# The stage before and in a selective scan: the convolution moved ahead of a norm, identity products in waits, and the scan taken quarter by quarter

## The chip, the cores and the metric

One core of a Trainium2 chip runs the whole kernel. The metric is the device time of one execution in microseconds (us), the median of three runs. TensorE multiplies matrices into PSUM, VectorE (DVE) and ScalarE (ACT) work elementwise, GpSimd (POOL) works elementwise in SBUF, and SyncE (SP) issues the DMAs.

## The reference, cut to what matters

Six blocks with a layer norm after each; only the first, a Mamba-like block over x of shape 2 x 256 x 128, is touched:

```python
xn = _ln(x, ln1_g, ln1_b);  xm = _ln(xn, ln_g, ln_b)
x1 = xm @ w1_w + w1_b
xc = silu(depthwise_conv3(x1))                 # over time, per channel
delta = softplus(xc @ dt_w + dt_b)             # [B, T, 128]
Bt, Ct = xc @ Bp_w + Bp_b, xc @ Cp_w + Cp_b    # [B, T, 16]
A = -exp(A_log)                                # [128, 16]
h = exp(delta * A) * h + delta * Bt * xc       # scan over T, 128 x 16 states
y = sum_n h * Ct + D_p * xc
mo = (y * silu(xm @ v1_w + v1_b)) @ w2_w + w2_b
```

The second block attends from x to a context of 2 x 512 x 128, which is normed on its own (`cx`, the norm `ctx`), transposed to `cxnT` and projected to keys and values.

## The kernel before, in words

There are 512 columns (2 batches by 256 steps) and 2048 states, taken as 16 groups (`NG`) of 128 rows. Group (q, i) holds 8 of the 128 channels with 16 states each: channels 32q + 8i to 32q + 8i + 7. The list `ORDER` gives the group of each scan step s.

**Ahead of the scan.** VectorE norms x twice (L773, L776, L783), GpSimd computing each norm's rstd with a power (L488, L490). VectorE then norms the context's eight tiles (`layernorm("ctx", ...)`), and after that computes the convolution in three instructions (L825, L826, L828). TensorE transposes x, multiplies by w1 and v1, transposes the context, and multiplies xc by dt, B and C. ScalarE evacuates (L584, L592), takes the two Silus (L595, L598), the Exp of A_log into `nA` (L599), and the softplus parts Abs, Exp, Ln (L604 to L606). VectorE forms delta (L835) and delta times x (L850), and splits each into three bfloat16 parts (L792 to L801). A quarter q of the channels is then stacked as 96 rows, a part under another (`quads`): quarters 0 and 1 by copies on VectorE (`quad`, L843, three copies for each of delta and dx), quarters 2 and 3 by 12 DMAs (L416), for which step 4 waits.

**A scan step s.** TensorE spreads delta and dx of the group from `quads` over 128 rows (`mm` with `sel_g`, L1190) into banks s % 2 and 2 + s % 2. ScalarE makes dA by Exp (L639). VectorE multiplies the spread dx by B in place (L861) and scans (L866). GpSimd multiplies by C (L509) into one of eight buffers of `hC`. The spread of delta waits for dA of step s - 2, that of dx for the scan of step s - 2. Behind the two spreads TensorE's queue holds, from step 2 on, one `values0`, four 128-column products of the next block, evacuated by ScalarE (L630).

**The sum over states.** `y_of(k)` multiplies four groups' hC by `sel_y` (128 rows to 32 columns of weights) into rows 32q to 32q + 31 of bank 4. The groups are those of `SUMMED[k]`. It stands in TensorE's queue behind the spreads of steps 8, 10 and 14, and the last one behind step 15. Then follow D_p (L870), the gate (L873), w2, the residual and the next norm.

Every float32 matmul shows as two records in the trace.

Of the kernel before, what the change touches and what calls it, by code (L numbers as in the profile page):

```python
# [23 lines left out]
P = 128  # L24
# [5 lines left out]
NC_TILES = B * CS // P  # L30
STATE = 16
GD = P // STATE
NG = D // GD
# [11 lines left out]
PARTS = 3  # L45
# [8 lines left out]
VEC = {}  # L54
# [16 lines left out]
def program(nc, a, out):  # L71
# [3 lines left out]
    with ctx:  # L75
        def sb(name, shape, dt=f32):
            return ctx.enter_context(nc.sbuf_tensor(name, shape, dt))
# [65 lines left out]
        def v(name, i=0, rows=P):  # L143
            at = VEC[name][0] + i
            return vec[0:rows, at:at + 1]

        def rv4(name):
# [95 lines left out]
        t1 = sb("t1", [P, 4, NJ, 8])  # L243
        pr1 = sb("pr1", [P, 2, NJ, 8])
        cmb = sb("cmb", [P, NJ, E1])
        hh = big2(0, [P, C1, N])
        hsh = big1(0, [P, SH, N])

# [22 lines left out]
        S = {k: sem(k) for k in (  # L271
            "w1_ps", "v1_ps", "x1p_done", "conv_done", "xc_done", "gate_done",
            "dt_ps", "z_done", "BC_ps", "BC_done", "negA", "lg_done", "delta_parts", "dx_parts",
            "delta_quads", "dx_quads", "late_quads",
            "spread_d", "spread_x", "dA_done", "dBx_done", "scan_done", "hC_done", "y_ps",
            "yv_done", "mo_ps", "res_ready", "x2_done", "ff_ps", "ff_act", "ff2_ps",
            "cxnT_ps", "cxnT_done",
# [22 lines left out]
        def own(eng, chain):  # L300
# [3 lines left out]
            def link(ins):  # L304
# [4 lines left out]

        ORDER = ([(q, i) for two in ((0, 1), (2, 3)) for i in range(2) for q in two]
                 + [(q, i) for i in (2, 3) for q in range(4)])

        SUMMED = ((0, 1, 4, 5), (2, 3, 6, 7), (8, 9, 10, 11), (12, 13, 14, 15))
        KEYS = {"a": T, "x": CS}

        AHEAD = {"a": 24, "x": 29}
# [70 lines left out]
        def _(sp):  # L389
# [19 lines left out]
            sp.dma_start(eb[:], a["eb"].partition_broadcast(P)).then_inc(ld["e1"], 16)  # L409


            for kind, parts in enumerate(("delta_parts", "dx_parts")):
                for q in (2, 3):
                    for i in range(PARTS):
                        sp.wait_ge(S[parts], i + 1)
                        sp.dma_start(quads[32 * i:32 * i + 32, kind, q, :],  # L416
                                     dparts[32 * q:32 * q + 32, kind, i, :]
                                     ).then_inc(S["late_quads"], 16)

            def spread_max(L):  # L420

# [47 lines left out]
        def _(pool):  # L469
# [32 lines left out]
            for s in range(NG):  # L502
                pool.wait_ge(S["scan_done"], s + 1)
                if s == 0:
                    pool.wait_ge(S["BC_done"], 2)
                if s >= 8:

                    pool.wait_ge(S["y_ps"], 1 if s < 10 else 2)
                nc.gpsimd.tensor_tensor(hC[:, s % 8, :], hs[:, s % 4, :], Cn[:],  # L509
                                        ALU.mult).then_inc(S["hC_done"], 1)  # L510
            root("ln2")
# [63 lines left out]
        def _(act):  # L575
            link = own(act, act_own)

            def to_cols(dst, bank, ready, done, scale=None, bias=None, n=1):

                act.wait_ge(S[ready], n)  # L580
                if scale is None:
                    nc.scalar.activation(dst, ps[:, bank, :], ACT.Copy).then_inc(S[done], 1)
                else:
                    nc.scalar.activation(dst, ps[:, bank, :], ACT.Identity, scale=scale,  # L584
                                         bias=bias).then_inc(S[done], 1)


            act.wait_ge(ld["vec"], 16)
            to_cols(xT[:], 0, "xT_ps", "xT_done", v("ln_g"), v("ln_b"), 1)
            act.wait_ge(S["w1_ps"], 1)  # L590
            act.wait_ge(consts, 9)
# [4 lines left out]
                                 ).then_inc(S["gate_done"], 1)  # L596
            act.wait_ge(S["conv_done"], 1)
            nc.scalar.activation(xc[:], cv[:, 0, :], ACT.Silu).then_inc(S["xc_done"], 1)  # L598
            link(nc.scalar.activation(nA[:, 0, :], vec[:, VEC["A_log"][0]:VEC["A_log"][0] + NG],  # L599
                                      ACT.Exp))  # L600
            nc.scalar.mul(nA[:, 1, :], nA[:, 0, :], -1.0).then_inc(S["negA"], 1)

            act.wait_ge(S["z_done"], 1)
            link(nc.scalar.activation(dtmp[:, 0, :], cv[:, 1, :], ACT.Abs))  # L604
            link(nc.scalar.activation(dtmp[:, 1, :], dtmp[:, 0, :], ACT.Exp, scale=-1.0))
            nc.scalar.activation(dtmp[:, 2, :], dtmp[:, 1, :], ACT.Ln, bias=1.0  # L606
                                 ).then_inc(S["lg_done"], 1)
# [6 lines left out]
            for i in range(2):  # L614
                to_cols(cxnT[:, i * 512:(i + 1) * 512], 6 + i, "cxnT_ps", "cxnT_done",
                        v("ctx_g"), v("ctx_b"), i + 1)
            act.wait_ge(S["negA"], 1)

            def evac0(c, kind):
# [145 lines left out]
        def _(dve):  # L765
            link = own(dve, dve_own)

            def layernorm(name, src, dst, meanwhile=None):

                k = NORMS.index(name)  # L770
                nt = src.shape[1]
                for j in range(nt):
                    ins = nc.vector.bn_stats(stats[:, j, :], src[:, j, :])  # L773
                link(ins)
                for j in range(nt):
                    ins = nc.vector.bn_aggr(meanvar[:, k, j, :], stats[:, j, :])  # L776
                ins.then_inc(norm_var, 1)
                dve.wait_ge(norm_var, k + 1)
                if meanwhile:
                    meanwhile()  # L780
                dve.wait_ge(norm_rstd, k + 1)
                for j in range(nt):
                    nc.vector.tensor_scalar(dst[:, j, :], src[:, j, :], meanvar[:, k, j, 0:1],  # L783
                                            rstd[:, k, j:j + 1], ALU.subtract, ALU.mult
                                            ).then_inc(norm_out, 1)
                dve.wait_ge(norm_out, normed_tiles(name))
# [16 lines left out]
            def gather_fours(L, fs=range(H // 4)):  # L803

                for f in fs:
                    for i in range(PARTS):
# [10 lines left out]
            layernorm("ln", summed[:], normed)  # L817

            dve.wait_ge(ld["cx"], 16)
            layernorm("ctx", cx, cx)  # L820

            dve.wait_ge(ld["vec"], 16)
            dve.wait_ge(S["x1p_done"], 1)
# [3 lines left out]
                                                cv3[:, 0], ALU.mult, ALU.add))  # L827
            nc.vector.scalar_tensor_tensor(cv3[:, 0], x1p[:, :, 2:T + 2], v("conv", 2), cv3[:, 1],  # L828
                                           ALU.mult, ALU.add).then_inc(S["conv_done"], 1)
            dve.wait_ge(S["dt_ps"], 1)  # L830
            nc.vector.tensor_scalar(cv[:, 1, :], ps[:, 3, :], v("dt_b"), None, ALU.add
                                    ).then_inc(S["z_done"], 1)
            dve.wait_ge(S["z_done"], 1)
            dve.wait_ge(S["lg_done"], 1)
            link(nc.vector.scalar_tensor_tensor(dl[:, 0, :], cv[:, 1, :], 0.0, dtmp[:, 2, :],  # L835
                                                ALU.max, ALU.add))
            split(dl[:, 0, :], [dparts[:, 0, i, :] for i in range(3)], dtmp[:, 0, :],
                  S["delta_parts"])

            def quad(kind, q, done):  # L840

                for i in range(PARTS):
                    ins = nc.vector.tensor_copy(quads[32 * i:32 * i + 32, kind, q, :],  # L843
                                                dparts[32 * q:32 * q + 32, kind, i, :])
                ins.then_inc(S[done], 1)

            dve.wait_ge(S["delta_parts"], PARTS)
            quad(0, 0, "delta_quads")
            dve.wait_ge(S["xc_done"], 1)
            link(nc.vector.tensor_tensor(dl[:, 1, :], dl[:, 0, :], xc[:], ALU.mult))  # L850
            split(dl[:, 1, :], [dparts[:, 1, i, :] for i in range(3)], dtmp[:, 1, :], S["dx_parts"])
            dve.wait_ge(S["dx_parts"], PARTS)
            quad(1, 0, "dx_quads")
            quad(0, 1, "delta_quads")
            quad(1, 1, "dx_quads")

            dve.wait_ge(S["BC_done"], 1)
            for s in range(NG):
# [329 lines left out]
        def _(pe):  # L1188
# [8 lines left out]
            def to_cols(bank, src, done, norm=None):  # L1197

                for j in range(NJ):
                    if norm:  # L1200
                        pe.wait_ge(norm_out, normed_tiles(norm, j))
                    ins = nc.tensor.transpose(ps[:, bank, j * P:(j + 1) * P], src[:, j, :], ident[:])  # L1202
                ins.then_inc(S[done], 1)
# [8 lines left out]


            pe.wait_ge(ld["ident"], 16)
            to_cols(0, normed, "xT_ps", "ln")
            pe.wait_ge(ld["mix"], 16)
            pe.wait_ge(S["xT_done"], 1)
            mm(ps[:, 1, :], w_mix[:, 0, :], xT[:]).then_inc(S["w1_ps"], 1)
            mm(ps[:, 2, :], w_mix[:, 1, :], xT[:]).then_inc(S["v1_ps"], 1)
            pe.wait_ge(norm_out, normed_tiles("ctx"))  # L1220
            for i in range(2):
                to_cols(6 + i, cx[:, 4 * i:4 * i + 4, :], "cxnT_ps")
            pe.wait_ge(S["xc_done"], 1)
            mm(ps[:, 3, :], w_mix[:, 2, :], xc[:]).then_inc(S["dt_ps"], 1)
            mm(ps[:, 4, :], w_mix[:, 3, :], xc[:])
            mm(ps[:, 5, :], w_mix[:, 4, :], xc[:]).then_inc(S["BC_ps"], 1)

            pe.wait_ge(ld["sel"], 32)
            pe.wait_ge(S["delta_parts"], PARTS)
# [46 lines left out]

            for s, (q, i) in enumerate(ORDER):
                if s >= 2:
                    pe.wait_ge(S["dA_done"], s - 1)
                if s < 2:  # L1280
                    pe.wait_ge(S["delta_quads"], s + 1)
                elif s == 4:
                    pe.wait_ge(S["late_quads"], 16 * 4 * PARTS)
                mm(ps[:, s % 2, :], sel_g[:, i, :], quads[:, 0, q, :]).then_inc(S["spread_d"], 1)
                if s < 2:
                    pe.wait_ge(S["dx_quads"], s + 1)
                if s >= 2:
                    pe.wait_ge(S["scan_done"], s - 1)
                mm(ps[:, 2 + s % 2, :], sel_g[:, i, :], quads[:, 1, q, :]
                   ).then_inc(S["spread_x"], 1)  # L1290
                if s in (8, 10, 14):
                    y_of((8, 10, 14).index(s))
                if s == 2:

                    pe.wait_ge(ld["x0"], 16)
                    pe.wait_ge(S["cxnT_done"], 2)
                if 0 <= s - 2 < V_EARLY:
                    values0((s - 2) // 2, s % 2)
# [479 lines left out]
```

## Time and profile before

| what | value |
|---|---|
| median of three runs | 533.27 us (531.43 to 534.46) |
| the profiled execution's own time | 532.46 us |
| span of the profile | 530.7 us |
| TensorE busy | 439.2 us (83%) |
| VectorE busy | 313.8 us (59%) |
| ScalarE busy | 205.0 us (39%) |
| GpSimd busy | 141.0 us (27%) |

The touched part runs from the start to about 75 us. The shares are averages over six blocks with different limits, so what matters here is the chain of waits of the first 75 us and the engines' timelines there. Granted clock is that of TensorE as a share of full speed, 0.50 being 1.2 GHz and 1.00 being 2.4 GHz.

### The profile page before, as it was taken

To read this page: it belongs to the slowest core of one execution; us is meant where nothing else is said; L and a number is where in the kernel's file an instruction comes from. 1 tells how busy PE (TensorE), PEld (TensorE's weight loads), DVE (VectorE), ACT (ScalarE), POOL (GpSimd) and SP (SyncE) were. 2 spreads that over 40 slices of the span, in tenths; PEclk is the share of its full clock that TensorE was granted. 3 is DMA by queue.
4 is the path that set the end of the run, shared out by engine and by line. 5 is a ranking of instruction groups with operands and counts; after the bars stand their busy time and mean duration, and the time that the engine had idled before them with its cause. 6 is when DMAs were issued, how large, how long until landed. Compare 5 with 4: busy or idle time off the path is not lost.

```text
span 530.7 us, 7338 instructions
## 1 busy us (share of the span) xinstructions
PE 439.2 (83%) x2780; PEld 265.4 (50%) x2788; DVE 313.8 (59%) x741; ACT 205.0 (39%) x257; POOL 141.0 (27%) x133
## 2 busy tenths in 40 slices
PE   0538978699999999889999888698567989978794
PEld 0206655354444445665777655345323544564384
DVE  4669954636766665542511487864696775236554
ACT  0555613143333233115333358774133444626500
POOL 3205643337767666400200400000100000003300
PEclk9867997989999999989999896999997999989898
DMA  8501000000004111060142230000000000010000
GB/s 305 214 25 44 2 1 0 1 2 1 0 1 158 41 41 40 19 228 1 60 64 31 49 61 0 3 3 1 0 3 0 2 2 3 1 31 0 0 1 20
DMA packets 7359, 19.37 MB, mean 37 GB/s; under 512 B 1750, under 2 KB 3126, under 8 KB 6806
## 3 DMA queue, kind: packets, MB, share of 16 engines
q1 hardware_dynamic: 7324, 18.91, 12.0%
q8 instruction: 22, 0.36, 0.3%
q14 instruction: 13, 0.11, 0.1%
HBM read 17.26 MB, written 1.15 MB: 35 GB/s over the span
## 4 chain that ended last, share of the span: by engine, by line
PE 40%; DVE 26%; POOL 15%; issue 13%; ACT 5%; DMA 1%; POOLq 0%; another core or an unknown queue 0%; DVEq 0%
PE ps L1190 38%; POOL big L540 7%; DVE ps L1043 4%; POOL big L547 4%; POOL rstd L490 2%; DVE ps L861 2%; DVE big L866 2%; DVE stats L773 2%; DVE mx_a L1047 2%; POOL big L522 2%; DVE normed L783 1%; ACT big L700 1%; PE ps L1202 1%; PE ps L1564 1%; DVE meanvar L776 1%
## 5 line engine op out<-in xcount | busy, mean ns | idle before, releaser
L1190 PE MATMUL ps<-big,late 128*32 128x256 f32 (+4 forms) x792 | 102.7, 386 | 12.4 <-DVE mx_x L1043 5.2
L1190 PE MATMUL ps<-late,big 128*128 128x128 f32 (+1 forms) x448 | 64.4, 276 | 3.6 <-DVE mx_x L1043 2.0
L1190 PEld LDWEIGHTS ps<-big,late 128*32 128x32 f32 (+3 forms) x800 | 39.5, 117 | 54.4 <-issue 23.1
L726 ACT ACTIVATE big<-ps 128x1024 f32<-128x1024 f32 x48 | 49.0, 1023 | 39.8 <-PE ps L1190 39.4
L488 POOL TENSOR_SCALAR vareps<-meanvar 128x4 f32<-128x4 f32 (+1 forms) x11 | 2.5, 229 | 221.1 <-DVE meanvar L776 221.1
L1190 PEld LDWEIGHTS ps<-late,big 128*128 128x128 f32 (+1 forms) x448 | 44.8, 152 | 27.4 <-issue 20.2
L664 ACT ACTIVATE big<-ps 128x1024 f32<-128x1024 f32 x32 | 32.8, 1024 | 64.8 <-PE ps L1190 47.0
L540 POOL TENSOR_TENSOR big<-big 128x512 f32<-128x512 f32 x32 | 40.5, 1267 | 43.2 <-DVE big L926 43.2
L1043 DVE CUSTOM_DVE_ANT_0 ps<-ps,big 128x512 f32<-128x512 f32 x64 | 42.5, 718 | 12.1 <-PE ps L1190 9.1
L1190 PE MATMUL ps<-big 64*128 64x256 f32 (+1 forms) x320 | 47.5, 410 | 1.7 <-POOL big L547 1.0
L926 DVE TENSOR_SCALAR big<-big 128x1024 f32<-128x1024 f32 x32 | 25.3, 790 | 39.7 <-ACT big L664 39.7
L1190 PEld LDWEIGHTS ps<-big 64*128 64x128 f32 (+1 forms) x320 | 27.9, 183 | 28.4 <-issue 22.8
L1190 PE MATMUL ps<-ctx_r,attn_w 128*128 128x512 f32 x64 | 33.4, 626 | 0.8 <-ACT late L630 0.8
L685 ACT ACTIVATE big<-ps 128x512 f32<-128x512 f32 x32 | 18.9, 597 | 29.0 <-PE ps L1190 29.0
L1190 PE MATMUL ps<-xT,late 128*128 128x512 f32 x64 | 29.0, 595 | 1.2 <-ACT big L685 1.2
L896 DVE TENSOR_TENSOR big<-ps,ctx_r 128x512 f32<-128x512 f32 x32 | 21.3, 685 | 12.8 <-PE ps L1190 12.7
L509 POOL TENSOR_TENSOR big<-big,mid 128x512 f32<-128x512 f32 x16 | 20.4, 1274 | 31.8 <-DVE big L866 31.8
L916 DVE RECIPROCAL big<-ps 128x256 f32<-128x256 f32 x16 | 28.0, 1747 | 1.3 <-PE ps L1190 1.3
L1190 PE MATMUL ps<-attn_w,big 128*128 128x128 f32 x192 | 26.3, 285 | 2.9 <-DVE big L917 2.3
L1190 PEld LDWEIGHTS ps<-attn_w,big 128*128 128x128 f32 x192 | 24.7, 197 | 6.3 <-DVE big L917 2.8
L1190 PEld LDWEIGHTS ps<-ident 128*128 128x128 f32 x212 | 25.6, 197 | 2.4 <-issue 2.3
L969 DVE SCALAR_TENSOR_TENSOR summed<-ps,g,summed 128x128 f32<-128x128 f32 x28 | 7.9, 344 | 31.5 <-PE ps L1190 31.5
(231 smaller groups left out, 686.0 us busy)
## 6 DMA issues: line engine op xcount, KB each, us to landing
attn_w<-in_w_x SPq DMA_DIRECT2D x1, 2560.0 KB, 13.2
big<-parts_kx SPq DMA_DIRECT2D x18, 128.0 KB
late<-in_w_up SPq DMA_DIRECT2D x1, 2048.0 KB, 7.7
late<-in_w_dn SPq DMA_DIRECT2D x4, 512.0 KB, 4.0
attn_w<-in_w_up SPq DMA_DIRECT2D x1, 1024.0 KB, 6.4
attn_w<-in_w_dn SPq DMA_DIRECT2D x1, 1024.0 KB, 9.3
parts_kx<-ctx_r SPq DMA_DIRECT2D x1, 768.0 KB, 4.4
rowv<-in_rowv SPq DMA_DIRECT2D x1, 576.0 KB, 3.8
```

Source lines behind the costliest of these rows:

```text
L490: nc.gpsimd.tensor_tensor(rstd[:, k, 0:nt], vareps[:, 0:nt], neghalf[:, 0:nt], ALU.pow).then_inc(norm_rstd, 1)
L509: nc.gpsimd.tensor_tensor(hC[:, s % 8, :], hs[:, s % 4, :], Cn[:], ALU.mult).then_inc(S["hC_done"], 1)
L540: nc.gpsimd.tensor_tensor(esum[:, s, :].rearrange("p (r t) -> p r t", r=2), e[:, :, 0, :], e[:, :, 1, :], ALU.add).then_inc(S["e0_sum"], 1)
L547: nc.gpsimd.tensor_tensor(etot[:, b, :], esum[:, 0, :], esum[:, 1, :], ALU.add).then_inc(S["e0_tot"], 1)
L664: nc.scalar.activation(ex[:, n % 3, :].rearrange("p (r n) -> p r n", r=2), ps[:, 2 * (n % 2):2 * (n % 2) + 2, :], ACT.Exp).then_inc(S["e0_ ...
L685: nc.scalar.activation(eh0[:, e % 2, c, :], ps[:, n % 3, :], ACT.Gelu).then_inc(S["up0_act"], 1)
L726: nc.scalar.activation(ex1[:, n % 3, :].rearrange("p (r n) -> p r n", r=2), ps[:, 2 * (n % 2):2 * (n % 2) + 2, :], ACT.Exp, scale=scale).t ...
L896: nc.vector.tensor_tensor(dst[:, n % 2, :], ps[:, 6 + i, :], rope0[:, i, :], ALU.mult).then_inc(S["k0_mul"], 1)
L916: link(nc.vector.reciprocal(dst, ps[:, 4 + b, T:2 * T]))
L926: nc.vector.tensor_scalar(ex[:, n % 3, :], ex[:, n % 3, :], float(np.exp(CLIP)), float(np.exp(-CLIP)), ALU.min, ALU.max).then_inc(S["e0_cl ...
L1043: nc.vector.tensor_tensor_reduce(ps[:, bank, :], ps[:, bank, :], mq[:, 2 * b + q, :], 1.0, -FAR, ALU.add, ALU.max, dst).then_inc(S[f"{L}_r ...
L1190: return nc.tensor.matmul(o, lhsT, rhs, start=start, stop=stop, skip_group_check=shared)
```

## The change

VectorE takes only statistics of the context, then the convolution, then the eight context tiles. ScalarE gets an Identity at its start, reads Abs from PSUM with dt_b as its bias, and computes `nA` after the context's evacuation. TensorE gets 20 identity products before the first transposes, 10 after w1 and v1, and 20 after the context's transposes, which now stand behind dt, B and C. VectorE stacks quarter 0 only; quarters 1 to 3 come by 18 DMAs, quarter 1 waited for at step 4 and the rest at step 8. The scan takes the four groups of a quarter one after the other, and the sums stand behind steps 6, 10, 14 and 15.

```diff
-        ORDER = ([(q, i) for two in ((0, 1), (2, 3)) for i in range(2) for q in two]
-                 + [(q, i) for i in (2, 3) for q in range(4)])
-        SUMMED = ((0, 1, 4, 5), (2, 3, 6, 7), (8, 9, 10, 11), (12, 13, 14, 15))
+        ORDER = [(q, i) for q in range(4) for i in range(4)]
+        SUMMED = ((0, 1, 2, 3), (4, 5, 6, 7), (8, 9, 10, 11), (12, 13, 14, 15))
...
-            for kind, parts in enumerate(("delta_parts", "dx_parts")):
-                for q in (2, 3):
+            for q in (1, 2, 3):
+                for kind, parts in enumerate(("delta_parts", "dx_parts")):
                     for i in range(PARTS):
                         sp.wait_ge(S[parts], i + 1)
                         sp.dma_start(quads[32 * i:32 * i + 32, kind, q, :],
                                      dparts[32 * q:32 * q + 32, kind, i, :]
-                                     ).then_inc(S["late_quads"], 16)
+                                     ).then_inc(S["second_quads" if q == 1 else "late_quads"], 16)
...
-                    pool.wait_ge(S["y_ps"], 1 if s < 10 else 2)
+                    pool.wait_ge(S["y_ps"], s // 4 - 1)
...
+            def set_table(function):
+                nc.scalar.activation(act_table[:], neghalf[:, 0:1], function)
             act.wait_ge(ld["vec"], 16)
+            act.wait_ge(consts, 1)
+            set_table(ACT.Identity)
...
-            link(nc.scalar.activation(nA[:, 0, :], vec[...A_log...], ACT.Exp))     # to behind cxnT
-            nc.scalar.mul(nA[:, 1, :], nA[:, 0, :], -1.0).then_inc(S["negA"], 1)   # to behind cxnT
+            act.wait_ge(S["dt_ps"], 1)
+            nc.scalar.activation(dtmp[:, 0, :], ps[:, 3, :], ACT.Abs, bias=v("dt_b")
+                                 ).then_inc(S["z_done"], 1)
             act.wait_ge(S["z_done"], 1)
-            link(nc.scalar.activation(dtmp[:, 0, :], cv[:, 1, :], ACT.Abs))
...
             dve.wait_ge(ld["cx"], 16)
-            layernorm("ctx", cx, cx)
+            (bn_stats and bn_aggr of the eight tiles of cx; norm_var)
             (the convolution: three instructions)
-            dve.wait_ge(S["dt_ps"], 1)
-            nc.vector.tensor_scalar(cv[:, 1, :], ps[:, 3, :], v("dt_b"), None, ALU.add
-                                    ).then_inc(S["z_done"], 1)
+            dve.wait_ge(norm_rstd, k_ctx + 1)
+            (the eight tiles of cx normed)
             dve.wait_ge(S["z_done"], 1)
+            link(nc.vector.tensor_scalar(cv[:, 1, :], ps[:, 3, :], v("dt_b"), None, ALU.add))
...
-            quad(1, 0, "dx_quads")
-            quad(0, 1, "delta_quads")
-            quad(1, 1, "dx_quads")
+            quad(1)
...
+            idle_work(3, 20)
             to_cols(0, normed, "xT_ps", "ln")
...
-            pe.wait_ge(norm_out, normed_tiles("ctx"))
-            for i in range(2):
-                to_cols(6 + i, cx[:, 4 * i:4 * i + 4, :], "cxnT_ps")
+            idle_work(3, 10)
             pe.wait_ge(S["xc_done"], 1)
             (dt, B and C)
+            pe.wait_ge(norm_out, normed_tiles("ctx"))
+            for i in range(2):
+                to_cols(6 + i, cx[:, 4 * i:4 * i + 4, :], "cxnT_ps")
+            idle_work(2, 20)
...
-                if s in (8, 10, 14):
-                    y_of((8, 10, 14).index(s))
+                if s in (6, 10, 14):
+                    y_of(s // 4 - 1)
```

## Rows read from the trace of the kernel before

**Rows 1.** Chain of waits, 0 to 110 us: start, us, what.

```profile
22.98 0.64 ACT mid L598
...
23.66 2.09 PE ps L1190 x2
...
27.87 1.28 ACT L606
...
29.85 0.47 issue
30.32 0.70 DVE mid L835
```

**Rows 2.** Timeline of TensorE: start, us, line, operation, count, idle before it.

```profile
53.55 1.06 PE L1190 MATMUL ps<-big,sel_y 128*32 128x512 f32 x8
...
55.54 0.60 PE L1190 MATMUL ps<-big,sel 96*128 96x512 bf16 x2
...
71.18 1.07 PE L1190 MATMUL ps<-big,sel_y 128*32 128x512 f32 x8 [1.29 <-POOL big L509]
...
74.84 1.88 PE L1190 MATMUL ps<-ctx_r,attn_w 128*128 128x512 f32 x4
...
96.74 2.39 PE L1190 MATMUL ps<-ident 128*128 128x128 f32 x20
```

**Rows 3.** Weight loads and matmuls of the state sums: min/median/max ns, start.

```profile
L1190 PEld LDWEIGHTS ps<-big,sel_y x32: 106/108/109, 53.5 to 71.2; 128*32 128x32 f32 x32
L1190 PE MATMUL ps<-big,sel_y x32: 592/604/617, 53.5 to 71.7; 128*32 128x512 f32 x32
```

**Rows 4.** Stretches of 2 us: engines' busy time, then granted clock, DMA.

```profile
24.00:26.00 2.00, 2.00 (x3) 0.83 (x3) 0.23 (x1) 1.34 (x3) 0.00 (x0) 0.50 0.00 0
...
74.00:76.00 2.00, 2.00 (x11) 1.41 (x12) 0.93 (x3) 0.00 (x0) 0.00 (x0) 1.00 0.00 0
```

**Rows 5.** Timeline of ScalarE.

```profile
13.74 1.28 ACT L584 ACT_TABLE_LOAD   x1 [13.74 <-PE ps L1202]
...
18.05 0.69 ACT L592 ACTIVATE mid<-ps,vec 128x512 f32<-128x512 f32 x1 [2.23 <-PE ps L1190]
```

**Rows 6.** Timeline of VectorE.

```profile
17.74 3.11 DVE L783 TENSOR_SCALAR ctx_r<-ctx_r,meanvar,rstd 128x128 f32<-128x128 f32 x8 [2.26 <-POOL rstd L490]
20.88 0.49 DVE L825 TENSOR_SCALAR cv<-mid,vec 128x512 f32<-128x512 f32 x1
...
37.42 2.69 DVE L843 COPY big<-mid 32x512 bf16<-32x512 bf16 x9
40.14 0.70 DVE L861 TENSOR_TENSOR ps<-ps,mid 128x512 f32<-128x512 f32 x1
...
56.78 0.67 DVE L861 TENSOR_TENSOR ps<-ps,mid 128x512 f32<-128x512 f32 x1
```

**Rows 7.** Timeline of GpSimd, at the start and in the router.

```profile
15.97 1.67 POOL L490 TENSOR_TENSOR rstd<-vareps,neghalf 128x8 f32<-128x8 f32 x1
17.71 1.26 POOL L500 TENSOR_TENSOR resid<-x,rowv 128x512 f32<-128x512 f32 x1
...
486.04 1.06 POOL L569 TENSOR_TENSOR big<-late 128x512 f32<-128x512 f32 x1 [0.61 <-ACT late L756]
```

**Rows 8.** VectorE in the router: one line's instructions (min/median/max ns), and one in the timeline.

```profile
L1128 DVE TENSOR_TENSOR pr<-late x5: 215/217/966, 484.1 to 487.4; 128x32 f32<-128x32 f32 x5
...
486.23 0.94 DVE L1128 TENSOR_TENSOR pr<-late 128x32 f32<-128x32 f32 x1
```

**Rows 9.** DMAs: those of L416 on SyncE, with their landing, and that of `ident`.

```profile
L416 SPq DMA_DIRECT2D big<-mid x12: 507/588/617, 31.5 to 39.2; - x12
...
DMA to landing us min/median/max: 1.8/1.8/1.9
...
L393 SPq DMA_DIRECT2D ident<-in_ident x1: 432/432/432, 2.1 to 2.1; - x1
...
DMA to landing us min/median/max: 3.7/3.7/3.7
```

More of the change, by code:

```diff
@@ L245, in program @@
         cmb = sb("cmb", [P, NJ, E1])
+        act_table = sb("act_table", [P, 1])
         hh = big2(0, [P, C1, N])
@@ L273, in program @@
             "dt_ps", "z_done", "BC_ps", "BC_done", "negA", "lg_done", "delta_parts", "dx_parts",
-            "delta_quads", "dx_quads", "late_quads",
+            "first_quads", "second_quads", "late_quads",
             "spread_d", "spread_x", "dA_done", "dBx_done", "scan_done", "hC_done", "y_ps",
@@ L598, in _ @@
             nc.scalar.activation(xc[:], cv[:, 0, :], ACT.Silu).then_inc(S["xc_done"], 1)
-            link(nc.scalar.activation(nA[:, 0, :], vec[:, VEC["A_log"][0]:VEC["A_log"][0] + NG],
-                                      ACT.Exp))
-            nc.scalar.mul(nA[:, 1, :], nA[:, 0, :], -1.0).then_inc(S["negA"], 1)
+            act.wait_ge(S["dt_ps"], 1)
+            nc.scalar.activation(dtmp[:, 0, :], ps[:, 3, :], ACT.Abs, bias=v("dt_b")
+                                 ).then_inc(S["z_done"], 1)
             act.wait_ge(S["z_done"], 1)
-            link(nc.scalar.activation(dtmp[:, 0, :], cv[:, 1, :], ACT.Abs))
             link(nc.scalar.activation(dtmp[:, 1, :], dtmp[:, 0, :], ACT.Exp, scale=-1.0))
@@ L616, in _ @@
                         v("ctx_g"), v("ctx_b"), i + 1)
+            link(nc.scalar.activation(nA[:, 0, :], vec[:, VEC["A_log"][0]:VEC["A_log"][0] + NG],
+                                      ACT.Exp))
+            nc.scalar.mul(nA[:, 1, :], nA[:, 0, :], -1.0).then_inc(S["negA"], 1)
             act.wait_ge(S["negA"], 1)
@@ L819, in _ @@
             dve.wait_ge(ld["cx"], 16)
-            layernorm("ctx", cx, cx)
+            k_ctx = NORMS.index("ctx")
+            for j in range(NC_TILES):
+                ins = nc.vector.bn_stats(stats[:, j, :], cx[:, j, :])
+            link(ins)
+            for j in range(NC_TILES):
+                ins = nc.vector.bn_aggr(meanvar[:, k_ctx, j, :], stats[:, j, :])
+            ins.then_inc(norm_var, 1)
+            dve.wait_ge(norm_var, k_ctx + 1)
             dve.wait_ge(ld["vec"], 16)
@@ L829, in _ @@
                                            ALU.mult, ALU.add).then_inc(S["conv_done"], 1)
-            dve.wait_ge(S["dt_ps"], 1)
-            nc.vector.tensor_scalar(cv[:, 1, :], ps[:, 3, :], v("dt_b"), None, ALU.add
-                                    ).then_inc(S["z_done"], 1)
+            dve.wait_ge(norm_rstd, k_ctx + 1)
+            for j in range(NC_TILES):
+                nc.vector.tensor_scalar(cx[:, j, :], cx[:, j, :], meanvar[:, k_ctx, j, 0:1],
+                                        rstd[:, k_ctx, j:j + 1], ALU.subtract, ALU.mult
+                                        ).then_inc(norm_out, 1)
+            dve.wait_ge(norm_out, normed_tiles("ctx"))
             dve.wait_ge(S["z_done"], 1)
+            link(nc.vector.tensor_scalar(cv[:, 1, :], ps[:, 3, :], v("dt_b"), None, ALU.add))
             dve.wait_ge(S["lg_done"], 1)
@@ L838, in _, with quad @@
                   S["delta_parts"])
-            def quad(kind, q, done):
+            def quad(kind):
                 for i in range(PARTS):
-                    ins = nc.vector.tensor_copy(quads[32 * i:32 * i + 32, kind, q, :],
-                                                dparts[32 * q:32 * q + 32, kind, i, :])
-                ins.then_inc(S[done], 1)
+                    ins = nc.vector.tensor_copy(quads[32 * i:32 * i + 32, kind, 0, :],
+                                                dparts[0:32, kind, i, :])
+                ins.then_inc(S["first_quads"], 1)
             dve.wait_ge(S["delta_parts"], PARTS)
-            quad(0, 0, "delta_quads")
+            quad(0)
             dve.wait_ge(S["xc_done"], 1)
@@ L1279, in _ @@
                     pe.wait_ge(S["dA_done"], s - 1)
-                if s < 2:
-                    pe.wait_ge(S["delta_quads"], s + 1)
+                if s == 0:
+                    pe.wait_ge(S["first_quads"], 1)
                 elif s == 4:
+                    pe.wait_ge(S["second_quads"], 16 * 2 * PARTS)
+                elif s == 8:
                     pe.wait_ge(S["late_quads"], 16 * 4 * PARTS)
                 mm(ps[:, s % 2, :], sel_g[:, i, :], quads[:, 0, q, :]).then_inc(S["spread_d"], 1)
-                if s < 2:
-                    pe.wait_ge(S["dx_quads"], s + 1)
+                if s == 0:
+                    pe.wait_ge(S["first_quads"], 2)
                 if s >= 2:
```

## The prediction

> **What bounds the kernel now.** I read the chain of waits over the first 110 us first. Up to the scan it is serial: VectorE's convolution behind the context's norm, a Silu, the product for delta at 23.66, Abs, Exp, a table load, Ln, and delta at 30.32 [rows 1]. Then I read the timelines engine by engine. On VectorE, after nine stacking copies, the first multiplication by B starts at 40.14, that of step 9 at 56.78, which is 1.85 us a step [rows 6]. The 16 steps follow without a gap, so VectorE sets the scan's pace and everything earlier counts one for one. TensorE is off the path in the scan but not idle: its queue carries two spreads and four other products each step, and a state sum now and then. Last I read the granted clock: 0.50 in the stretch with the delta product, 1.00 in the later one [rows 4]. The same form costs 2.09 us for two records at the one and 1.88 us for four at the other [rows 1, 2], so about 1.07 us for a whole product at full clock (start to start 0.43 to 0.47 a record, the last one 0.6 long).
>
> So the change has two halves: how much sooner the scan starts, and what its new order costs inside.
>
> **First half: up to the scan.**
>
> *The table load.* The 1.28 us load ahead of L584 stands behind the transposes on TensorE [rows 5]. Set in a wait it is free. xT is then ready at about 14.5, w1 at 15.6 (full clock) or 16.6 (half), and x1p, which takes 0.69 us [rows 5], at 16.3 or 17.3. Before, x1p began at 18.05.
>
> *The convolution.* It no longer waits for the norm of 3.11 us [rows 6], and alone (0.49, 0.75 and 0.75 with their gaps: 2.06 us) would end at 18.4, against 22.94 before, just ahead of the Silu at 22.98 [rows 1]. But GpSimd's power runs until 17.64 and its 1.26 us residual add follows at 17.71 [rows 7]. In the router a 32-element addition with two SBUF inputs, 217 ns in the median, takes 0.94 us when it starts inside a GpSimd add of 1.06 us, ending with it [rows 7, 8]. The context's first tile starts beside the residual add and is late too: eight tiles take 3.11 us [rows 6] where 2.2 would do. L825 then ends at about 18.1, the residual add at 19.4, L826 at 20.15, L828 at 20.9. The gain is 2.0 us, if the power blocks as the adds do, which no row shows. If nothing blocks it is 4.5. I take 2.0, the value nearest to rows in which GpSimd blocks VectorE.
>
> The Trainium skill (SBUF — State Buffer, "Who interferes with whom") has the rule: GpSimd holds a port pair shared with VectorE for its whole instruction, and a fast-mode or two-SBUF-input VectorE instruction waits. By that rule the power blocks as well and the gain is the 2.0 just given; the router rows agree with it.
>
> *The delta product.* The identity products may bring it to full clock: 1.07 for 2.09 us, 1.0 gained. At half clock, nothing. Ten products take 20 records, 2.39 us at full clock [rows 2]; the ten after v1 end by 20, before xc at 21.5, and even at half clock cost at most a microsecond. The 20 at the start begin when `ident` lands at 5.8 [rows 9] and need 4.8 to 9.6 us, for transposes that VectorE feeds until 13.1. I take 1.0.
>
> *Softplus.* VectorE's addition (0.75 us) leaves the path. But the Exp table, formerly loaded in a wait for `nA`, is now loaded behind Abs: 1.28 us on the path, the price of Ln's load [rows 1]. Net a loss of 0.5. The 0.47 us between Ln and L835 [rows 1] I leave.
>
> For that load the Trainium skill (ScalarE: Activation LUTs, "What ACT_TABLE_LOAD costs") gives 2.66 us, the load plus a drain. By that figure this step would lose 1.4 us more. The rows show Ln starting right behind 1.28 us, so the trace does not show the drain.
>
> *Stacking.* Six of the nine copies (2.69 us [rows 6]) go: 1.8 us. The first dx spread, until now hidden by them, comes onto the path at 0.4 to 0.6 us with its hand-over. Net gain 1.1. The price is 18 DMAs in place of 12 at 0.59 us each [rows 9]: quarter 1 lands 1.8 us after the last dx part, over 4 us before step 4; the other twelve are issued in some 7 us more and land about 5 us before step 8. Hidden. The context load behind them on SyncE is needed a block later.
>
> *The other moves.* Context norm, transposes and `nA` fit in the waits for softplus and splitting: the transposes end near 25.5 and the 20 products (4.8 us at full clock) near 30.3, before the first spread at 31.5. ScalarE reaches the end of `nA` (load included) at about 31.4, in time.
>
> Sum: 2.0 + 1.0 - 0.5 + 1.1 = **3.6 us sooner**. Bounds: 2.6 (half clock) and 6.1 (no blocking).
>
> **Second half: the scan's order.** In a sum before, eight records of about 0.6 us each take 1.06 us in all [rows 2, 3]. The four groups of `SUMMED` there have four different q, so they write four different blocks of 32 rows, and the eight records run side by side. After the change all four have one q: same columns of the array, accumulating in the same rows of bank 4. They can't run side by side. Eight records at 0.43 start to start and 0.6 for the last make 3.6 us; **each sum costs 2.55 us more**. If each record's weight load were exposed, at 0.108 us [rows 3], add 0.85.
>
> The Trainium skill (TensorE: Matmul & The Clock Gate, "Part 3: Packing small matmuls") says the same against this change: small outputs overlap when each lands in its own column group. The trace agrees with the side-by-side half; the serial half no row of this kernel shows.
>
> What that does to VectorE: in the step after a sum, the spreads at 55.54 take 0.60 and end at 56.14; the multiplication that needs them starts at 56.78 [rows 2, 6]. So the slack is 0.64, and a sum behind a step's spreads and ahead of the next ones delays VectorE by 2.55 - 0.64 = 1.9 us. (dA, which needs its Exp too, has about 0.84.) One step later TensorE has caught up, since its spreads and products fill only 1.3 us of a step's 1.85. So three sums inside the scan cost 3 x 1.9 = 5.7 us. The fourth stands on the path by itself, from GpSimd's last product at 71.18 on [rows 2]: 2.55 us more. Together **8.25 us lost**, up to 11.6 with weight loads exposed.
>
> **Sum.** 8.25 - 3.6 = 4.65 us slower, on the profiled execution's own time of 532.46 us: 537.1. That execution stands 0.8 below the median of 533.27; taken on the median the sum gives 537.9. I put the forecast between, at 537.5 us.
>
> **The rivals.**
>
> *A. Faster: the sums don't wait for one another.* Then the early gain stands alone: 532.9 - 3.6, about 529 us. For it: TensorE's queue has 0.5 us spare a step, and if four sums run in 1.06 us as before, nothing in the scan moves. Against it: same array columns, same output rows. It decides if a sum takes under 1.7 us, when its growth stays inside the 0.64 us slack. 0.12.
>
> *B. About no change: more is gained early.* With no port wait at the convolution the gain is 6.1 and the loss still 8.25: 535.0 us; a downstream product meeting a better clock by a microsecond or two would do the same. For it: no row shows the power blocking. 0.24.
>
> *C. My forecast*, serial sums and a blocked convolution, 535.9 to 540.5: 0.56.
>
> *D. Still slower: the identity products stand in the way.* The 20 behind the context's transposes precede the first spread. At half clock they take 9.6 us and end near 35 to 36, 4 us late: about 541.5 us. It decides from about 6 us for the 20. Against it: TensorE has work nearly without a pause from the delta product on, and the 20 records at 96.74, which follow other products, run at full speed [rows 2]. Exposed weight loads end near there too. 0.08.
>
> **How the numbers follow.** A change of 0.5%, 2.7 us, is about what a measurement of this kernel can tell from none. Faster holds A: 0.12. Same holds B: 0.24. Slower holds C and D: 0.64. The range runs from 533.5 (B, with a little to spare) to 540.5 (C with most of the weight loads exposed); it leaves out A and nearly all of D.
>
> **What would show it.** Records of the sums: eight with starts 0.43 apart and 3.6 us in all, at four places. VectorE: gaps of near 2 us before the multiplication by B of steps 7, 11 and 15, none elsewhere. The first such multiplication near 36.5 in place of 40.14. L825 longer than 0.49 and L826 or L828 longer than 0.75. A 1.28 us load between Abs and Exp. The prediction is wrong if a sum takes near 1.1 us, if the gaps at 7, 11 and 15 are absent, or if the first spread waits for identity products.

## The result, and the profile after

The changed kernel takes 537.29 us in the median of four runs (536.71 to 537.6), against 532.57 us for four runs of the kernel before: a ratio of 1.0084 (95% interval 1.0051 to 1.0117). It is slower, by 4.7 us; its profiled execution took 537.6 us, 5.1 more than that of before, with a span of 535.8. One of e5_no_idle's eight executions took 748.86 us at a granted clock of 0.56, and its ratio below leaves it out.

The chain of waits from the first multiplication by B to D_p, in the changed kernel (start, us, what):

```profile
34.41 0.62 PE ps L1206
...
35.12 0.71 DVE ps L877
...
37.13 12.86 PE ps L1206 x59
...
50.01 0.71 DVE ps L877
...
53.87 5.48 PE ps L1206 x19
...
63.23 5.48 PE ps L1206 x19
...
70.76 1.27 POOL big L509
...
72.08 3.63 PE ps L1206 x8
...
75.73 0.76 DVE cv L886
```

The scan begins 5.0 us sooner, at 35.12 in place of 40.14 [rows 6], yet D_p starts at 75.73, where before it started at 72.31:

```profile
72.31 0.75 DVE L870 SCALAR_TENSOR_TENSOR cv<-mid,vec,ps 128x512 f32<-128x512 f32 x1 [2.53 <-PE ps L1190]
```

And the scan's chain, which ran along VectorE, now runs along TensorE for long pieces. TensorE's timeline shows what it does there, and what it did first:

```profile
6.19 6.73 PE L1206 MATMUL ps<-ident 128*128 128x128 f32 x40 [6.19 <-DMA ident<-in_ident]
12.76 0.61 PE L1218 MATMUL ps<-ident,normed 128*128 128x128 f32 x4
14.33 1.96 PE L1206 MATMUL ps<-xT,w_mix 128*128 128x512 f32 x4 [0.96 <-ACT xT L584]
...
20.11 2.84 PE L1206 MATMUL ps<-mid,w_mix 128*128 128x512 f32 x6 [1.59 <-ACT mid L604]
...
23.66 4.63 PE L1206 MATMUL ps<-ident 128*128 128x128 f32 x40
...
44.13 0.77 PE L1206 MATMUL ps<-big,sel 96*128 96x512 bf16 x2
44.83 3.62 PE L1206 MATMUL ps<-big,sel_y 128*32 128x512 f32 x8
48.38 1.16 PE L1206 MATMUL ps<-attn_w,ctx_r 128*128 128x128 f32 x8
49.38 0.60 PE L1206 MATMUL ps<-big,sel 96*128 96x512 bf16 x2
...
72.08 3.62 PE L1206 MATMUL ps<-big,sel_y 128*32 128x512 f32 x8 [0.71 <-POOL big L509]
```

Each state sum takes 3.62 us for the same eight records that took 1.06 and 1.07 before [rows 2]. The spreads behind the first one come at 49.38, and VectorE waits for them. Its timeline, with the idle time in brackets:

```profile
44.37 0.67 DVE L877 TENSOR_TENSOR ps<-ps,mid 128x512 f32<-128x512 f32 x1
...
46.22 0.67 DVE L877 TENSOR_TENSOR ps<-ps,mid 128x512 f32<-128x512 f32 x1
...
50.01 0.70 DVE L877 TENSOR_TENSOR ps<-ps,mid 128x512 f32<-128x512 f32 x1 [1.87 <-PE ps L1206]
...
59.37 0.70 DVE L877 TENSOR_TENSOR ps<-ps,mid 128x512 f32<-128x512 f32 x1 [1.86 <-PE ps L1206]
...
68.72 0.70 DVE L877 TENSOR_TENSOR ps<-ps,mid 128x512 f32<-128x512 f32 x1 [1.86 <-PE ps L1206]
...
75.73 0.75 DVE L886 SCALAR_TENSOR_TENSOR cv<-mid,vec,ps 128x512 f32<-128x512 f32 x1 [5.06 <-PE ps L1206]
```

The idle times stand before steps 7, 11 and 15, each behind a sum. The step from 46.22 to 50.01 is 3.79 us long, where 44.37 to 46.22 is 1.85.

### The profile page after: what moved, and what is told of

Same layout as the page of the kernel before. It is cut to its first block, busy times and chain, and to the rows that moved or that the text cites. A ratio compares the mean times of both kernels' runs of the same rounds, so it can differ in the third digit from the quotient of the medians.

```text
span 535.8 us, 7539 instructions
## 1 busy us (share of the span) xinstructions
PE 458.4 (86%) x2880; PEld 278.9 (52%) x2888; DVE 311.8 (58%) x735; ACT 205.0 (38%) x258; POOL 141.1 (26%) x133
## 4 chain that ended last, share of the span: by engine, by line
PE 46%; DVE 22%; POOL 14%; issue 11%; ACT 5%; DMA 1%; SPq 0%; POOLq 0%; another core or an unknown queue 0%; DVEq 0%
PE ps L1206 43%; POOL big L540 7%; DVE ps L1059 4%; POOL big L547 4%; DVE mx_a L1063 2%; POOL big L522 1%; POOL rstd L490 1%; DVE big L882 1%; ACT big L707 1%; DVE normed L790 1%; PE ps L1218 1%; DVE stats L780 1%; DVE ps L877 1%; PE ps L1585 1%; DMA ident<-in_ident 1%
## 5 line engine op out<-in xcount | busy, mean ns | idle before, releaser
L1206 PEld LDWEIGHTS ps<-late,big 128*128 128x128 f32 (+1 forms) x448 | 45.0, 152 | 28.3 <-issue 20.2
L540 POOL TENSOR_TENSOR big<-big 128x512 f32<-128x512 f32 x32 | 40.6, 1268 | 43.3 <-DVE big L942 43.3
L1206 PE MATMUL ps<-ident 128*128 128x128 f32 x312 | 40.2, 288 | 6.2 <-DMA ident<-in_ident 6.2
L1206 PEld LDWEIGHTS ps<-ident 128*128 128x128 f32 x312 | 39.1, 205 | 9.1 <-DMA ident<-in_ident 6.2
```

The source lines that it names most:

```text
L540: nc.gpsimd.tensor_tensor(esum[:, s, :].rearrange("p (r t) -> p r t", r=2), e[:, :, 0, :], e[:, :, 1, :], ALU.add).then_inc(S["e0_sum"], 1)
L1206: return nc.tensor.matmul(o, lhsT, rhs, start=start, stop=stop, skip_group_check=shared)
```

## The experiments

All ratios are to the kernel before run on the same chip (its medians there were 532.6 to 534.0 us), with 95% intervals; times and scan starts of different runs also differ by some tenths from when the first DMAs land. For each run "scan start" is the first multiplication by B, and "D_p" the start of that instruction.

| run | median us | ratio (interval) | scan start | D_p | D_p to the end of the span |
|---|---|---|---|---|---|
| before | 532.57 | | 40.14 | 72.31 | 458.4 |
| changed | 537.29 | 1.0084 (1.0051 to 1.0117) | 35.12 | 75.73 | 460.1 |
| e1_mixed_sums | 527.62 | 0.9893 (0.9874 to 0.9912) | 35.19 | 67.37 | 458.0 |
| e2_side_by_side | 528.05 | 0.9883 (0.9856 to 0.9910) | 35.59 | 67.93 | 459.6 |
| e3_only_order | 541.84 | 1.0142 (1.0120 to 1.0164) | 40.11 | 80.74 | 459.7 |
| e4_late_add | 535.82 | 1.0057 (1.0037 to 1.0078) | 34.59 | 75.53 | 457.6 |
| e5_no_idle | 537.21 | 1.0084 (1.0058 to 1.0110) | 36.95 | 77.86 | 457.5 |
| e6_exp_set | 536.32 | 1.0067 (1.0041 to 1.0093) | 34.04 | 75.02 | 457.6 |
| e7_all | 527.47 | 0.9881 (0.9853 to 0.9910) | 32.98 | 65.86 | 459.8 |
| e8_all_12 | 525.92 | 0.9868 (0.9846 to 0.9889) | 33.80 | 65.97 | 457.6 |

### e1: the sums over four quarters again

```diff
-        ORDER = [(q, i) for q in range(4) for i in range(4)]
-        SUMMED = ((0, 1, 2, 3), (4, 5, 6, 7), (8, 9, 10, 11), (12, 13, 14, 15))
+        ORDER = [(0, 0), (0, 1), (1, 0), (1, 1), (2, 0), (3, 0), (2, 1), (3, 1)] + [
+            (q, i) for i in (2, 3) for q in range(4)]
+        SUMMED = ((0, 2, 4, 5), (1, 3, 6, 7), (8, 9, 10, 11), (12, 13, 14, 15))
...
-            for q in (1, 2, 3):
-                for kind, parts in enumerate(("delta_parts", "dx_parts")):
+            for kind, parts in enumerate(("delta_parts", "dx_parts")):
+                for q in (1, 2, 3):
...
-                    pool.wait_ge(S["y_ps"], s // 4 - 1)
+                    pool.wait_ge(S["y_ps"], 1 if s < 9 else 2)
...
-    (second_quads waited for at step 4, late_quads at step 8; sums behind steps 6, 10, 14)
+    (second_quads waited for at step 2, late_quads at step 4; sums behind steps 8, 10, 14)
```

> The changed kernel with a scan order in which each sum again takes its four groups from four quarters, though quarter 0 alone is needed for steps 0 and 1. Theory (four sums of one quarter each run their records one after the other, 3.62 us in place of 1.06): the sums fall back to near 1.06 us, the gaps of 1.9 us on VectorE at steps 7, 11 and 15 go, the scan's start stays near 35.1. 3 x 1.94 + 2.55 = 8.4 us less than the changed kernel: about 529 us, a ratio to the kernel before of 0.993. Rival (the gaps come from the stacks by DMA, or from the start being so early that TensorE's other products crowd the queue): the gaps stay, or move to steps 2 and 4 where the stacks are now waited for, and the time stays within 2 us of 537.

527.62 us. The state sums' records in this run (min/median/max ns, first and last start), and VectorE's last multiplication by B and D_p:

```profile
L1207 PE MATMUL ps<-big,sel_y x32: 592/605/617, 48.6 to 66.7; 128*32 128x512 f32 x32
```

```profile
62.91 0.67 DVE L878 TENSOR_TENSOR ps<-ps,mid 128x512 f32<-128x512 f32 x1
...
67.37 0.75 DVE L887 SCALAR_TENSOR_TENSOR cv<-mid,vec,ps 128x512 f32<-128x512 f32 x1 [2.53 <-PE ps L1207]
```

From 35.19 to 62.91 are 15 steps of 1.85 us: no gap is left, and the stacks waited for at steps 2 and 4 are in time. Scan start to D_p is 32.2 us, as before (32.2), where the changed kernel takes 40.6: 8.4 us, as the theory had it. The rival falls. The ratio, 0.989, is lower than the 0.993 expected: the median is 9.7 us below the changed kernel's, and of this the part ahead of D_p explains 8.4 (the part behind D_p is taken up further down).

### e2: the same order, each product into rows of its own

```diff
-                    ins = mm(ps[32 * q:32 * q + 32, 4, :], sel_y[:, i, :], hC[:, s % 8, :],
-                             i == 0, i == 3)
+                    ins = mm(ps[32 * i:32 * i + 32, 4, :], sel_y[:, i, :], hC[:, s % 8, :],
+                             True, True)
```

> The changed kernel with its scan order, places and counts untouched, but each of a sum's four products writes rows of its own, 32i to 32i+31, in place of adding into 32q to 32q+31; the sum over the four groups of a quarter is left out, so the state sums are wrong and everything behind them too. Theory (the array's columns are what the four products contend for): each sum takes about 1.06 us again, no gap at steps 7, 11, 15, 8.4 us less than the changed kernel: about 529 us. Rival (the order of the scan or the earlier place of the sum in the queue delays VectorE, not the array columns): the sums still take 3.6 us or the gaps stay, and the time stays near 537.

Order, places in the queue, count of matmuls and their operands are the changed kernel's; the output rows differ, and with them nothing is added up over the four groups. The last of the sums, and D_p:

```profile
66.80 1.07 PE L1206 MATMUL ps<-big,sel_y 128*32 128x512 f32 x8 [1.29 <-POOL big L509]
```

```profile
67.93 0.75 DVE L886 SCALAR_TENSOR_TENSOR cv<-mid,vec,ps 128x512 f32<-128x512 f32 x1 [2.53 <-PE ps L1206]
```

The three sums inside the scan take 1.07, 1.06 and 1.06 us, VectorE has no gap at steps 7, 11 and 15, D_p comes 32.3 us after the scan start, and the median is 528.05. So neither the order of the scan nor the earlier place of the sums costs anything; having four products of one sum in the same 32 rows does. The run also settles a second rival. Before the change the four products of a sum shared one `i`, and so the same weights `sel_y[:, i, :]`, while the changed kernel takes four different ones. e2 takes four different ones too, and its sums are fast.

Whether it is the array's columns or the accumulation in the same rows that makes them wait was not parted: the edit changes both. A hint for the columns is that w1 and v1, which fill all columns but write different banks, also follow one another: four records in 1.96 us in the changed kernel, about 0.45 us apart.

### e3: the order alone, on the kernel before

```diff
-        ORDER = ([(q, i) for two in ((0, 1), (2, 3)) for i in range(2) for q in two]
-                 + [(q, i) for i in (2, 3) for q in range(4)])
-        SUMMED = ((0, 1, 4, 5), (2, 3, 6, 7), (8, 9, 10, 11), (12, 13, 14, 15))
+        ORDER = [(q, i) for q in range(4) for i in range(4)]
+        SUMMED = ((0, 1, 2, 3), (4, 5, 6, 7), (8, 9, 10, 11), (12, 13, 14, 15))
...
-                if s in (8, 10, 14):
-                    y_of((8, 10, 14).index(s))
+                if s in (6, 10, 14):
+                    y_of(s // 4 - 1)
```

> The kernel before with the change's scan order and its sums alone; the early part, its stacks and waits are those of before (quarter 1 waited for at step 4, quarters 2 and 3 at step 8). Theory: the scan starts near 40.1 as before, plus three gaps of 1.9 us and 2.55 us at the end: 8.4 us slower than the kernel before, about 541 us, ratio 1.016. Rival (the sums delay VectorE only because the scan now starts early, beside the cold clock and the late stacks): gaps smaller than 1 us, ratio below 1.008.

The waits for the stacks and for the buffers of `hC` are moved to fit the order. 541.84 us, scan start 40.11, D_p at 80.74, with the same gaps of VectorE:

```profile
55.01 0.70 DVE L860 TENSOR_TENSOR ps<-ps,mid 128x512 f32<-128x512 f32 x1 [1.86 <-PE ps L1189]
...
64.37 0.70 DVE L860 TENSOR_TENSOR ps<-ps,mid 128x512 f32<-128x512 f32 x1 [1.86 <-PE ps L1189]
...
73.73 0.70 DVE L860 TENSOR_TENSOR ps<-ps,mid 128x512 f32<-128x512 f32 x1 [1.87 <-PE ps L1189]
```

The loss does not need the early start. With e1 and e3 the change falls into two halves measured apart: the early part gains (ratio 0.989, with the sums mended), the order loses (1.014). At D_p the two add up: 4.9 us sooner in e1 and 8.4 later in e3 make 3.5 later, and 3.4 was measured. The ratios do not add up so well (0.989 times 1.014 is 1.003, against 1.008), since they hold the part behind D_p as well.

### e4: the residual add after the context's norm

```diff
             pool.wait_ge(ld["rowv"], 16)
+            pool.wait_ge(norm_out, normed_tiles("ctx"))
             nc.gpsimd.tensor_tensor(resid[:], x[:], rv4("w2_b"), ALU.add)
```

> The changed kernel with GpSimd's first residual add waiting until the context is normed. Theory (this add blocks the convolution's third instruction, 1.80 us in place of 0.75): L842 takes 0.75, the Silu of the convolution begins 1.05 us sooner, the scan begins 1.0 us sooner, near 34.1, the end comes about 1 us sooner. Rival (its length is VectorE's own, from waiting for the scalar or for ScalarE's write): it stays at 1.80. A second one: the power blocks too once the add is away; L839 or L840 lengthen.

VectorE in the changed kernel, and then in this one:

```profile
16.28 0.49 DVE L839 TENSOR_SCALAR cv<-mid,vec 128x512 f32<-128x512 f32 x1 [0.95 <-ACT mid L598]
16.80 0.75 DVE L840 SCALAR_TENSOR_TENSOR cv<-mid,vec,cv 128x512 f32<-128x512 f32 x1
17.59 1.80 DVE L842 SCALAR_TENSOR_TENSOR cv<-mid,vec,cv 128x512 f32<-128x512 f32 x1
```

```profile
16.79 0.49 DVE L840 TENSOR_SCALAR cv<-mid,vec 128x512 f32<-128x512 f32 x1 [1.36 <-ACT mid L599]
17.31 0.75 DVE L841 SCALAR_TENSOR_TENSOR cv<-mid,vec,cv 128x512 f32<-128x512 f32 x1
18.10 0.75 DVE L843 SCALAR_TENSOR_TENSOR cv<-mid,vec,cv 128x512 f32<-128x512 f32 x1
```

GpSimd in the two, in the same order:

```profile
15.83 1.67 POOL L490 TENSOR_TENSOR rstd<-vareps,neghalf 128x8 f32<-128x8 f32 x1
17.57 1.27 POOL L500 TENSOR_TENSOR resid<-x,rowv 128x512 f32<-128x512 f32 x1
```

```profile
15.91 1.67 POOL L490 TENSOR_TENSOR rstd<-vareps,neghalf 128x8 f32<-128x8 f32 x1
21.07 1.27 POOL L501 TENSOR_TENSOR resid<-x,rowv 128x512 f32<-128x512 f32 x1 [3.49 <-DVE ctx_r L847]
```

The third instruction takes 0.75 us once the add is away: the add was what held it, for 1.05 us. The power, which ends at 17.50 in the changed kernel, held neither of the first two: L840 began at 16.80, 0.70 us before that end, and was done at 17.55. The third, which the add did hold, needed 0.55 us more after the add's end at 18.84. The scan start moved only 0.5 us in place of the 1.0 expected, since in this execution the convolution began 0.5 us later: `ident` landed at 6.74 in place of 6.19, and the 20 identity products in front of the transposes ended that much later. At D_p only 0.2 us are left (the waits at steps 4 and 7 grew by 0.1 and 0.2); the rest of the lower median is not the edit's, since the part behind D_p took 457.6 us in place of 460.1.

### e5: no identity products

```diff
-            idle_work(3, 20)
...
-            idle_work(3, 10)
...
-            idle_work(2, 20)
```

> The changed kernel without the 50 identity products of the early part. Theory: the delta product runs at half clock, 2.1 us in place of 1.14, and the w1 product too, about 2.1 in place of 1.1; VectorE's convolution begins 1 us later and falls wholly behind the residual add, so the scan begins 2 us later, near 37, and the time rises by 1 to 2 us to 538.5 to 539.5. Rival (they do nothing, or the 20 at the start cost as much by holding the transposes back): scan start and time within 0.5 us of the changed kernel.

The two products that follow xT, and delta, B and C, in this run:

```profile
14.41 3.75 PE L1206 MATMUL ps<-xT,w_mix 128*128 128x512 f32 x4 [0.96 <-ACT xT L584]
...
20.97 5.49 PE L1206 MATMUL ps<-mid,w_mix 128*128 128x512 f32 x6 [2.81 <-ACT mid L604]
```

They took 1.96 and 2.84 us in the changed kernel (four and six records). The scan starts 1.8 us later: x1p 1.0 later, then delta's product 1.0 longer, less 0.2 in the collision with the add. So the products do what they are for. But the median, 537.21, is the changed kernel's, because the part behind D_p took 457.5 us against 460.1 in the profiled executions. On the time the expectation (538.5 or more) missed.

### e6: the Exp table behind the Silu

```diff
             nc.scalar.activation(xc[:], cv[:, 0, :], ACT.Silu).then_inc(S["xc_done"], 1)
+            set_table(ACT.Exp)
             act.wait_ge(S["dt_ps"], 1)
```

> The changed kernel with a one-column Exp behind the convolution's Silu, so that the Exp table is loaded while TensorE makes the delta product. Theory (the 1.28 us load behind Abs is on the path): it moves into the wait of 1.2 us there, Abs may begin up to 0.3 us later, delta comes 1.0 us sooner, the scan begins near 34.1. Rival (Abs is not in the Exp table's set beside PSUM input, or another load appears): nothing gained.

ScalarE in the changed kernel, and then in this one:

```profile
21.27 0.69 ACT L606 ACTIVATE dtmp<-ps,vec 128x512 f32<-128x512 f32 x1 [1.22 <-PE ps L1206]
21.97 1.28 ACT L609 ACT_TABLE_LOAD   x1
23.27 0.63 ACT L609 ACTIVATE dtmp<-dtmp 128x512 f32<-128x512 f32 x1
```

```profile
20.07 1.28 ACT L590 ACT_TABLE_LOAD   x1
21.37 0.20 ACT L590 ACTIVATE act_table<-neghalf 128x1 f32<-128x1 f32 x1
21.48 0.67 ACT L607 ACTIVATE dtmp<-ps,vec 128x512 f32<-128x512 f32 x1
22.18 0.63 ACT L610 ACTIVATE dtmp<-dtmp 128x512 f32<-128x512 f32 x1
```

Abs starts 0.2 later, Exp 1.1 sooner, and the scan 1.1 sooner (34.04 for 35.12). The load behind Abs was on the path at its whole 1.28 us. At D_p 0.7 us are left.

### e7: the three edits together

> The changed kernel with three edits together: sums over four quarters, the residual add behind the context's norm, the Exp table set early. If the three add up: 8.4 + 1.0 + 1.0 = 10.4 us less than the changed kernel, about 527 us, ratio to the kernel before 0.989, scan start near 33. If the parts overlap (the stacks of quarters 1 to 3 come too late for an earlier start, or the identity products then hold the first spread back): a gap at step 2 or 4, and 528 us or more.

The scan starts at 32.98, 2.1 us sooner, so the two small edits add up there. But step 4 now waits:

```profile
41.08 0.70 DVE L880 TENSOR_TENSOR ps<-ps,mid 128x512 f32<-128x512 f32 x1 [0.61 <-PE ps L1209]
```

TensorE had waited 1.19 us at 34.91 for the DMA of quarter 1's stack, and its products ran at half speed there. D_p comes 9.9 us sooner than in the changed kernel; the median is 527.47, a ratio no different from that of e1 within their intervals.

### e8: 12 identity products in place of 20 at the start

```diff
-            idle_work(3, 20)
+            idle_work(3, 12)
```

> The kernel with the three edits together, and 12 identity products at its start in place of 20. The 20 end at 12.4 to 13.4 us, depending on when the identity's DMA lands, and the first transposes, ready from 12 us on, wait for them. Theory (that wait is on the path when the DMA lands late): 12 products end near 11, xT no longer depends on the DMA's landing, w1 still runs at full clock, and the scan starts 0 to 0.6 us sooner than with 20 (32.98), never later. Rival (fewer products leave the clock at half): the w1 product takes 2.1 us in place of 1.1 and the scan starts 1 us later, as without any products. The time: within 1 us of 527.5 either way, since the part behind the scan varies by 2 us between executions.

TensorE's start in this run, and its granted clock (the column before the last two) around it:

```profile
6.09 5.49 PE L1209 MATMUL ps<-ident 128*128 128x128 f32 x24 [6.09 <-DMA ident<-in_ident]
12.41 1.10 PE L1221 MATMUL ps<-ident,normed 128*128 128x128 f32 x4 [0.82 <-DVE normed L793]
14.46 3.11 PE L1209 MATMUL ps<-xT,w_mix 128*128 128x512 f32 x4 [0.96 <-ACT xT L586]
```

```profile
12.00:14.00 2.00, 1.10 (x4) 0.55 (x4) 1.96 (x9) 0.46 (x1) 0.00 (x0) 1.00 1.10 473
14.00:16.00 2.00, 1.54 (x3) 0.82 (x4) 1.44 (x13) 0.41 (x2) 0.28 (x2) 0.78 0.95 410
16.00:18.00 2.00, 2.00 (x5) 0.96 (x4) 1.24 (x2) 1.97 (x3) 1.62 (x1) 0.50 0.93 367
```

The rival held in the main: the clock fell to 0.50 during the w1 product, and the scan starts at 33.80, 0.8 later than with 20. "Never later" was wrong. The w1 product itself cost less than the rival said, since x1p began only 0.46 us later than in e7 (15.91 for 15.45). The rest came from the ten identity products behind v1: begun at half clock, they ran from 17.37 to 20.32, the Silu was done at 19.45, and delta's product stood behind them until 20.16. The later start cost nothing at D_p (65.97 for 65.86), since step 4 no longer waits, and the median of 525.92, which lies outside the expected 1 us around 527.5, is the lowest of all; it is 1.3% below the kernel before, and its interval overlaps those of e1 and e7, so which of the three is best is not settled.

## Why the prediction was right

The forecast was 537.5 us, slower, and 537.29 was measured. Step by step, changed kernel less kernel before:

| term | predicted | in the profiles | how read |
|---|---|---|---|
| convolution's end | 2.0 sooner | 3.55 sooner | 19.39 for 22.94, of which 0.15 is x landing sooner |
| delta's product | 1.0 | 0.95 | 1.14 for 2.09 |
| softplus | -0.5 | -0.54 | product's end to L853: 5.11 for 4.57 |
| stacking | 1.1 | 1.06 | delta to scan start: 8.76 for 9.82 |
| early part | 3.6 sooner | 5.0 sooner | 35.12 for 40.14 |
| three sums in the scan | 5.7 later | 5.8 | 3 x (3.79 - 1.85) |
| the last sum | 2.55 later | 2.55 | 3.62 for 1.07 |
| the scan with its last sum | 8.25 later | 8.4 later | 40.6 for 32.2 |
| net at D_p | 4.65 later | 3.4 later | 75.73 for 72.31 |
| behind D_p | 0 | 1.7 later | 460.1 for 458.4 |

**The order of the scan** was the part that decided, and both its price a sum and VectorE's slack of 0.64 us held to 0.05 us. e1 and e3 show its effect from both sides, e2 that it comes from the four products' output rows.

**The convolution** was sized too small. The prediction had the power block L825 (now L839) as the adds do, and that step failed: L839 took its 0.49 us and L840 its usual 0.75, and the convolution ended at 19.39 in place of the 20.9 forecast. The residual add did block as forecast, for 1.05 us. The rule of the Trainium skill (SBUF — State Buffer, "Who interferes with whom") is that a GpSimd instruction which reads SBUF holds the pair for its whole length against a VectorE instruction with two SBUF inputs. The rows of the changed kernel, shown under e4, go against it for the power: L840 was done 0.05 us after the power's end, though 0.70 us of it lay beside the power. They agree with it for the add.

**Stacking** came out at 1.06 us for 1.1, but the prediction's own terms, 1.8 less 0.4 to 0.6, give 1.2 to 1.4. The first spread kept VectorE waiting for 0.77 us, more than was put down for it, so this hit is in part luck.

**Behind D_p** the forecast had nothing, and 1.7 us came. They sit in three stretches: 0.8 in the feed-forward (its first three products take 5.46 us for 4.74), 0.3 up to the end of the mixture of experts, and 0.6 between there and the next norm. The second is a gain of 0.6 us in the attention and a loss of 0.9 behind it. None of these stretches' code changed. Over the ten kernels the part behind D_p takes 457.5 to 460.1 us, with no relation to what was edited: e2 and e7 have 460 with fast sums, e5 has 457.5 without identity products. It does go with TensorE's speed in the feed-forward. Put in order of the time of its first three products, the ten profiled executions stand in the order of the part behind D_p too, but for differences of 0.1 us: 4.32 to 4.41 us in e5, e4, e6 and e8 (457.5 to 457.6), 4.60 in e1 (458.0), 4.74 before (458.4), 5.19 to 5.46 in e3, e2, e7 and the changed kernel (459.6 to 460.1). Over these products the granted clock of the kernel before was 0.50 up to 86.5 us and 0.79 from there to 88.0; in the changed kernel it was 0.50 from 86.53 to 92.0. So the clock's late return is the likely cause. What sets the moment of its return no run tested, and the remaining differences behind the feed-forward were not traced. So the near hit of 0.2 us owes something to two misses of 1.4 and 1.7 us that cancel, and an error of 1 to 2 us was to be expected either way.

**The rivals.** A (sums not waiting for one another) fell to the 3.62 us rows. B (more gained early) had its mechanism right for the power alone, 1.4 us of its 2.5; the residual add did block. D (identity products in the way of the first spread) fell: the 40 records at 23.66 end at 28.3, and the first spread waits for its stack until 30.49. Another form of it was seen, though: the 20 at the start can hold the transposes. In e4 `ident` landed at 6.74 and the evacuation of xT began 0.5 us later than in the changed kernel. In e2 `ident` landed at 5.93, sooner than there, but the 40 records took 7.62 us in place of 6.73, and the evacuation began 0.6 us later.

**The other steps.** Quarter 1's stack was in time for step 4 in the changed kernel. ScalarE finished `nA` at 30.1, before the first spread. The table load behind Abs cost its 1.28 us and no drain showed, as in the kernel before. The 2.66 us that the Trainium skill gives (ScalarE: Activation LUTs, "What ACT_TABLE_LOAD costs") did not appear here.

## What to carry to other kernels

Here, products with 32 columns of weights were cheap only as long as neighbours in the queue wrote different blocks of 32 rows: before reordering a loop, look at which output rows become neighbours. One reorder turned 1.06 us into 3.62 four times. TensorE was not the bound, but VectorE had only 0.64 us of slack, so each of the three sums inside the scan cost it 1.9 us, and the fourth cost its whole 2.55. The gain was to be had without the loss: keep the first two steps in one quarter, and let each sum still take four (e1, 1.1% faster than before).

## What was not expected of the hardware

- GpSimd's power on 128 x 8 elements, 1.67 us long, did not hold up the two VectorE instructions that ran beside it, while its add on 128 x 512 elements, 1.27 us long, held an instruction with two SBUF inputs for 1.05 us (1.80 for 0.75).
- With 24 identity records at the start and 0.8 us of idle time behind them, the granted clock fell from 1.00 to 0.50 within the w1 product (e8); with 40 it stayed high, and w1 and v1 together took 1.96 in place of 3.11 us.
- The profile's granted clock reads 1.00 in e5 around 14 to 18 us while four records take 3.75 us, where they take 1.96 in the changed kernel, and the first value below 1.00 comes in the stretch from 30 to 32 us. Ahead of the first change that such a trace shows, the length of a known record told more here than that column.
